# Weight loads placed between the activation loads in a projection, attention and feed-forward kernel on eight cores

## The chip, the cores and the metric

The program runs on all 8 NeuronCores of one Trainium2 chip, four on each of its two dies. Every core runs the same instructions on its own half of a batch entry. The metric is the device time of the slowest core in microseconds (us). Each core has five engines, called here PE (matmuls), DVE (vector), ACT (activations), POOL and SP; SP does no arithmetic and issues most of the transfers.

## The reference, cut to what matters

```python
def attn(x, Wqk_w, Wqk_b, Wv_w, Wv_b, Wo_w, Wo_b):      # x: (4, 4096, 4096), seen as 8 heads of 64
    qk = (x @ Wqk_w.T + Wqk_b).reshape(b, n, H, E, 2)
    q, k = qk[..., 0], qk[..., 1]                       # heads in front
    v = (x @ Wv_w.T + Wv_b).reshape(b, n, H, E)
    scores = einsum('bhqd,bhkd->bhqk', q, k)
    attn = softmax(scores, axis=-1) / sqrt(512)
    out = einsum('bhsl,bhlv->bhsv', attn, v)
    return out @ Wo_w.T + Wo_b
x = layernorm(x + attn(x))
x = layernorm(x + ffn(x))     # ffn: x @ W_base.T + b_base, plus 8 low-rank experts of which 2 are mixed in
```

## The kernel before, in words

A core holds one batch entry: all 4096 tokens for keys and values, and 2048 of them for queries and for everything behind the attention. Activations lie transposed, with the 4096 features along the partitions in 32 chunks of 128.

The kernel writes its program through a small recording layer (class Sched, line 56). `s.op(engine, function, waits, dma=stream)` appends an instruction to the engine's list, in the order in which the Python code comes to it, and puts semaphore waits in front of it. An engine works through its list in that order, so an instruction of SP that waits holds up every transfer that SP issues behind it. A DMA stream ("ld", "sc", three semaphores each) also makes a transfer wait for the third one before it in that stream. `Res` keeps who wrote and who reads a buffer. `phase_barrier` (line 73) ends a stage: all engines meet, and the next stage's first instructions wait for all transfers.

The stages that the change touches, in order:

- **Keys** (lines 306 to 386). The weight wkT comes first, by `wload` (line 199): 32 loads of 256 KB by SP (line 208) into two staging buffers `wstg`, each cast to bf16 by DVE (line 214) into `wk_bf`. Then, for 16 groups of 256 tokens and 8 groups of 4 feature chunks, SP loads x (line 331, 512 KB, three buffers `xstg`), POOL or ACT in turn casts it (lines 343 and 338), ACT sends the cast to the scratch tensor xscr in memory (line 348), and PE does 16 matmuls with it. One pass over the 8 groups is a contraction; ACT then moves its result to `kT` (line 381).
- **Values** (lines 390 to 457). The same with wvT: 16 loads of 512 KB into two buffers, cast by DVE; then 16 passes of 8 loads of 256 KB from xscr (line 416) and 64 matmuls.
- **Queries** (lines 461 to 518). 16 loads of wqT as for the values; then 4 passes of 8 loads of 512 KB (line 480) and 128 matmuls.
- **Attention** (lines 522 to 837). First SP loads the output weight woT in 16 pieces of 512 KB through one buffer `wstgo` (line 548); POOL casts each (line 555) to `wo_bf`. Then come 16 groups (4 head pairs by 4 groups of 512 queries). For each query the maximum of its scores is found first: PE computes scores `sS`, DVE reduces them (line 593), PE transposes the maxima (line 618), DVE writes them as rows `mrow` and `mtmp` (line 631), and SP copies `mtmp` to partition 64 of `mrow` (line 647). Then PE computes the scores again into `rb`, adds the negative maxima by a matmul with `mrow`, ACT takes the exponential (line 739), and PE multiplies by the values. The score and maximum work of the next group (list `units`) is handed out in small pieces between the steps of the present one (`drain_n`); what is left of it is issued by `drain_until` when the next group begins.

`wo_bf` is read only in the stage after the attention. The feed-forward stages behind it are not touched.

## Time and profile before

| What | us |
|---|---|
| time, median of 2 runs (lowest to highest) | 4124.35 (4116.83 to 4131.87) |
| the profiled execution, its own time | 4120.41 |
| span of its slowest core, core 7 (first to last instruction) | 4117.0 |
| span of its fastest core, core 4 | 4054.7 |
| PE busy on core 7 | 3156.3 (77%) |
| DVE, ACT and POOL busy | 1401.7, 829.5, 671.2 |

The rows come from one profiled execution, on core 7 unless the group says otherwise. Times count from the span's start. PEld is PE's weight load, which runs beside its matmuls. In the slices the span is cut into 40 equal parts, and each digit is the busy share in tenths. In the rows of stretches PEclk is the share of its full clock that PE was granted, and the DMA share is the mean of the core's 16 DMA engines. A name like "SPq" stands for issuing a transfer on SP's queue; the transfer itself lands later.

### The profile page before, as it was taken

The page shows a single profiled execution, that of the slowest core. Times are in us where ns is not written, and L with a number is a line of the kernel's source. Part 1 is how long each engine was busy: PE and PEld are TensorE (multiplying, and loading weights), DVE is VectorE, ACT ScalarE, POOL GpSimd, SP SyncE. Part 2 cuts the span into 40 slices and gives each one's busy share as a digit, 9 for nine tenths or more (in the row PEclk, how much of TensorE's full clock was granted, in tenths as well). Part 3 has the DMA queues.
Part 4 walks back from the last instruction along what each step waited for, and adds up shares of the span by engine and source line. Part 5 has one row for each costly group of instructions (what it writes and reads, how often), then busy time and mean ns, then how long its engine had stood idle before and what let it go on. Part 6 is the DMA issues. An engine that isn't in the chain of part 4 may idle for free.

```text
span 4117.0 us, 46517 instructions; the slowest of 8 cores (4054.7 to 4117.0 us)
## 1 busy us (share of the span) xinstructions
PE 3156.3 (77%) x13476; PEld 1181.6 (29%) x13476; DVE 1401.7 (34%) x1972; ACT 829.5 (20%) x1412; POOL 671.2 (16%) x543
## 2 busy tenths in 40 slices
PE   2766499586888887888888887742899997999950
PEld 1555234231222221222212222111344442444420
DVE  1000100115666666565655637771100002111123
ACT  0222000001333333333333343220000000000000
POOL 0111000001000000000000003453222212444425
PEclk9999799795777766777866779986899998999975
DMA  6999544432000000000000012316454536677737
GB/s 180 278 278 278 178 133 136 156 123 62 1 1 1 4 1 1 3 1 1 1 3 1 1 49 96 104 58 184 129 160 146 159 105 194 205 203 209 204 112 184
DMA packets 451280, 444.76 MB, mean 108 GB/s; under 512 B 22112, under 2 KB 403169, under 8 KB 451042
## 3 DMA queue, kind: packets, MB, share of 16 engines
q1 hardware_dynamic: 348130, 341.12, 28.5%
q10 hardware_dynamic: 102912, 100.68, 7.8%
q8 instruction: 123, 2.02, 0.2%
q14 instruction: 115, 0.94, 0.1%
HBM read 340.01 MB, written 100.66 MB: 107 GB/s over the span
## 4 chain that ended last, share of the span: by engine, by line
PE 54%; DVE 8%; issue 6%; DMA 5%; POOL 3%; SPq 0%; ACT 0%; DVEq 0%; POOLq 0%; ACTq 0%
PE pf L155 24%; PE sS L155 10%; PE rb L155 9%; PE a L155 7%; DVE racc L593 3%; DMA res2d<-r2scr 2%; DVE x2g L997 2%; POOL tmpf L987 2%; PE po L155 2%; DMA wstgo<-woT 1%; POOL tmpo L1137 1%; PE pss L155 1%; PE sS L618 1%; PE psq L155 1%; DVE res L934 1%
## 5 line engine op out<-in xcount | busy, mean ns | idle before, releaser
L155 PE MATMUL pf<-x2h,wqf 128*128 128x512 bf16 x4096 | 909.1, 380 | 5.8 <-DVE hs L1333 5.8
L593 DVE TENSOR_REDUCE racc<-sS 128x1 f32<-128x512 f32 x1024 | 682.0, 689 | 529.3 <-PE sS L155 517.9
L739 ACT ACTIVATE probs<-rb 128x512 bf16<-128x512 f32 x1024 | 543.4, 600 | 914.4 <-PE rb L155 910.4
L155 PE MATMUL sS<-kT,qT 64*128 64x512 bf16 x1024 | 476.0, 483 | 152.5 <-DVE racc L593 115.7
L155 PEld LDWEIGHTS pf<-x2h,wqf 128*128 128x128 bf16 x4096 | 396.6, 98 | 505.1 <-issue 38.5
L987 POOL TENSOR_TENSOR tmpf<-res,abc 128x512 f32<-128x512 bf16 x128 | 158.5, 1254 | 1653.8 <-DVE abc L968 1599.5
L155 PE MATMUL pk<-xbf,wk_bf 128*128 128x256 bf16 x2048 | 254.9, 277 | 177.9 <-POOL xbf L343 103.9
L1424 DVE SCALAR_TENSOR_TENSOR res2c<-pf,bB_sb,x2h 128x1024 bf16<-128x1024 f32 x64 | 82.2, 1284 | 864.4 <-PE pss L155 781.2
L1358 POOL CAST wqf<-wstgf 128x1024 bf16<-128x1024 f32 x256 | 264.5, 1040 | 613.6 <-DMA wstgf<-wbT 450.0
L155 PE MATMUL a<-probs,V 128*65 128x512 bf16 x1024 | 363.1, 480 | 0.0
L155 PE MATMUL rb<-qT,kT 64*128 64x512 bf16 x1024 | 337.9, 472 | 0.2
L155 PE MATMUL rb<-mrow,ones 1*128 1x512 bf16 x1024 | 246.6, 468 | 41.0 <-DMA mrow<-mtmp 41.0
L155 PE MATMUL pv<-wv_bf,xvb 128*128 128x512 bf16 x1024 | 229.8, 382 | 62.7 <-DMA xvb<-xscr 47.7
L155 PEld LDWEIGHTS pk<-xbf,wk_bf 128*128 128x128 bf16 x2048 | 195.1, 99 | 237.5 <-issue 210.6
L1442 ACT ACTIVATE sqc<-res2c 128x1024 bf16<-128x1024 bf16 x64 | 67.7, 1058 | 951.7 <-DVE res2c L1424 923.2
L155 PEld LDWEIGHTS sS<-kT,qT 64*128 64x128 bf16 x1024 | 98.0, 96 | 510.2 <-issue 506.2
L155 PE MATMUL po<-OT,wo_bf 128*128 128x512 bf16 x512 | 141.6, 406 | 69.9 <-DVE res L934 64.2
L1137 POOL TENSOR_TENSOR tmpo<-res2d,a 128x1024 f32<-128x1024 bf16 x64 | 155.0, 2439 | 241.3 <-DMA res2d<-r2scr 126.4
L155 PEld LDWEIGHTS a<-probs,V 128*65 128x65 bf16 x1024 | 107.2, 130 | 172.8 <-issue 149.1
L155 PE MATMUL pq<-xqb,wq_bf 128*128 128x512 bf16 x512 | 116.2, 388 | 51.8 <-DMA xqb<-xscr 47.0
L155 PEld LDWEIGHTS pv<-wv_bf,xvb 128*128 128x128 bf16 x1024 | 99.0, 98 | 193.3 <-issue 84.9
L997 DVE TENSOR_TENSOR x2g<-tmpf,bbc 128x512 bf16<-128x512 f32 x128 | 141.2, 1134 | 34.0 <-POOL tmpf L987 33.5
(104 smaller groups left out, 1603.8 us busy)
## 6 DMA issues: line engine op xcount, KB each, us to landing
wstgf<-wbT SPq DMA_DIRECT2D x256, 512.0 KB
xstg<-xrot SPq DMA_DIRECT2D x128, 512.0 KB
xscr<-xbf ACTq DMA_DIRECT2D x128, 256.0 KB, 5.5
xvb<-xscr SPq DMA_DIRECT2D x128, 256.0 KB, 2.8
outT<-outst ACTq DMA_DIRECT2D x64, 512.0 KB, 5.4
xqb<-xscr SPq DMA_DIRECT2D x32, 512.0 KB, 3.7
xq<-xscr SPq DMA_DIRECT2D x32, 512.0 KB, 3.9
x2scr<-x2g ACTq DMA_DIRECT2D x32, 512.0 KB, 2.8
```

The lines of the kernel that those rows point to most:

```text
L155: return lambda e: e.matmul(o, l, r, start=st, stop=sp, skip_group_check=True)
L593: e.reduce_max(d, srd, AX.X, negate=True),
L618: idn=id32[:]: e.transpose(o, i, idn),
L739: e.activation(d, srd, AF.Exp),
L934: e.scalar_tensor_tensor(d, a, b, c2, ALU.add, ALU.add),
L987: e.tensor_tensor(d, a, b, ALU.mult),
L997: e.tensor_tensor(d, a, b, ALU.add),
L1137: b=a2[:]: e.tensor_tensor(d, a, b, ALU.mult),
L1358: e.tensor_copy(d, srd),
L1424: e.scalar_tensor_tensor(d, a, b, c2, ALU.add, ALU.add),
L1442: e.activation(d, a, AF.Square),
```

## The change

`wjobs` does what `wload` did, but returns a list of functions, each of which records one load and its cast. The activation loops call four of these after every activation load until the list is empty, so that the 32 weight loads stand between the first 8 activation loads of each projection. The staging buffers become three of 256 KB each in all three projections; for values and queries that makes 32 loads out of 16. The weight of the keys uses the stream "sc" (its x loads use "ld"), those of values and queries "ld". The 16 loads of woT become a list too, and one is recorded at the start of each attention group.

```diff
+    def wjobs(dst_bf, dstR_list, src_dram, stg, stgR, n_chunks, cw,
+              eng="DVE", dma="ld"):
+        src_r = src_dram.ap().rearrange("(c p) n -> p c n", p=128)
+        per = stg[0].shape[1] // cw
+        nb = len(stg)
+
+        def mk(g):
+            def f():
+                st_i = g % nb
+                src = src_r[:, per * g:per * g + per, :]
+                tl = s.op("SP", lambda e, d=stg[st_i], src=src, per=per:
+                          e.dma_start(d.ap().rearrange(
+                              "p (c n) -> p c n", c=per), src),
+                          waits=stgR[st_i].wr(), dma=dma)
+                stgR[st_i].did_write(tl)
+                tc = s.op(eng,
...
+                          waits=[tl])
+                stgR[st_i].did_read(tc)
+                for j in range(per):
+                    dstR_list[per * g + j].did_write(tc)
+            return f
+        return [mk(g) for g in range(n_chunks // per)]
...
-                    wstg = [sbP("wstg%d" % i, [128, 512], F32) for i in range(2)]
-                    wstgR = [Res(), Res()]
+                    wstg = [sbP("wstg%d" % i, [128, 512], F32) for i in range(3)]
+                    wstgR = [Res(), Res(), Res()]
...
-                    wload(wk_bf, wkR, wkT, wstg, wstgR, 32, 512,
-                          eng="DVE", stripe=True)
+                    wkj = wjobs(wk_bf, wkR, wkT, wstg, wstgR, 32, 512,
+                                eng="DVE", dma="sc")
...
                                 xstgR[bi].did_write(tl)
+                                for _ in range(4):
+                                    if wkj:
+                                        wkj.pop(0)()
...
-                    wstg = [sbP("wstgv%d" % i, [128, 1024], F32) for i in range(2)]
-                    wstgR = [Res(), Res()]
+                    wstg = [sbP("wstgv%d" % i, [128, 512], F32) for i in range(3)]
+                    wstgR = [Res(), Res(), Res()]
...
-                    for hh in range(4):
-                        for c in range(4):
-                            st_i = 0
+                    def mk_woj(hh, c):
+                        def f():
...
+                        return f
+                    woj = [mk_woj(hh, c) for hh in range(4) for c in range(4)]
...
                             for qg in range(4):
+                                if woj:
+                                    woj.pop(0)()
                                 drain_until(hp * 4 + qg)
```

The values and queries get the same edits as the keys, with `wvj` and `wqj`.

On SP's queue the start of the key stage reads as follows before; wstg is the staging of the weight wkT, xstg that of the activations.

```order
L242 DMA epsc<-c_eps 1x1
L208 DMA wstg<-wkT 128x512 x32
L331 DMA xstg<-xrot 128x4x256 x128
L140 UNCONDITIONAL_BRANCH
L151 UNCONDITIONAL_BRANCH
```

And so with the change; the pair of rows repeats eight times.

```order
L268 DMA epsc<-c_eps 1x1
L357 DMA xstg<-xrot 128x4x256
L231 DMA wstg<-wkT 128x512 x4
...
L357 DMA xstg<-xrot 128x4x256 x120
L140 UNCONDITIONAL_BRANCH
```

All 32 weight loads stood ahead of the first activation load; now an activation load comes first and four weight loads follow each of the first eight. In the value and query stages SP's queue has the same new pattern, with xvb and xqb in the place of xstg.

On SP's queue the attention stage begins as follows before; wstgo is the staging of woT, and mrow<-mtmp is the row of maxima that PE waits for.

```order
L151 UNCONDITIONAL_BRANCH
L548 DMA wstgo<-woT 128x1024 x16
L647 DMA mrow<-mtmp 1x16x32 x4
L833 DMA OT<-OTtmp 64x2048
L647 DMA mrow<-mtmp 1x16x32 x4
```

And so with the change, from the start of the stage to the first transfer behind the first head pair.

```order
L151 UNCONDITIONAL_BRANCH
L582 DMA wstgo<-woT 128x1024
L683 DMA mrow<-mtmp 1x16x32
L582 DMA wstgo<-woT 128x1024
L683 DMA mrow<-mtmp 1x16x32
...
L871 DMA OT<-OTtmp 64x2048
```

One load of woT stands ahead of each mrow transfer, where all 16 stood ahead of the first.

## Rows read from the trace of the kernel before

**Rows 1.** The span in 40 slices: busy tenths of PE and of the DMA engines.

```profile
PE   2766499586888887888888887742899997999950
DMA  6999544432000000000000012316454536677737
```

**Rows 2.** Busy time by stretches of the first three stages.

```profile
core 7: us, PE busy (x) PEld busy (x) DVE busy (x) ACT busy (x) POOL busy (x), PEclk, DMA share, GB/s
20.00:60.00 40.00, 0.00 (x0) 0.00 (x0) 9.82 (x23) 0.00 (x0) 0.00 (x0) 1.00 0.50 151
60.00:80.00 20.00, 8.97 (x64) 6.90 (x64) 1.28 (x3) 3.40 (x3) 3.12 (x3) 1.00 0.84 240
160.00:360.00 200.00, 140.44 (x1141) 107.13 (x1140) 0.00 (x0) 51.19 (x71) 37.45 (x36) 0.99 0.98 279
440.00:472.00 32.00, 0.00 (x0) 0.00 (x0) 9.02 (x13) 0.00 (x0) 0.00 (x0) 0.50 0.61 199
540.00:700.00 160.00, 150.51 (x677) 64.02 (x676) 0.00 (x0) 10.90 (x20) 0.00 (x0) 1.00 0.47 135
...
820.00:900.00 80.00, 77.52 (x357) 34.66 (x356) 0.00 (x0) 4.86 (x8) 0.00 (x0) 1.00 0.44 138
```

**Rows 3.** Timeline of the key stage: start us, us, what [idle before <-releaser].

```profile
9.10 53.55 SPq L208 DMA_DIRECT2D wstg<-wkT  x32
...
62.70 64.45 SPq L331 DMA_DIRECT2D xstg<-xrot  x24
...
66.84 0.43 DVE L214 CAST wk_bf<-wstg 128x512 bf16<-128x512 f32 x1 [2.38 <-DMA wstg<-wkT]
68.27 1.04 POOL L343 CAST xbf<-xstg 128x1024 bf16<-128x1024 f32 x1 [56.91 <-DMA xstg<-xrot]
...
69.56 7.06 PE L155 MATMUL pk<-xbf,wk_bf 128*128 128x256 bf16 x48 [69.56 <-POOL xbf L343]
...
92.31 0.93 PE L155 MATMUL pk<-xbf,wk_bf 128*128 128x256 bf16 x7
```

**Rows 4.** DMA issues: operation, count, KB each, median us to landing.

```profile
wstg<-wkT SPq DMA_DIRECT2D x32, 256.0 KB, 2.8
wstgv<-wvT SPq DMA_DIRECT2D x16, 512.0 KB, 4.4
...
mrow<-mtmp SPq DMA_DIRECT2D x16, 1.0 KB, 1.6
```

**Rows 5.** Timeline of the value stage's start.

```profile
435.13 38.09 SPq L208 DMA_DIRECT2D wstgv<-wvT  x16
...
479.81 15.33 PE L155 MATMUL pv<-wv_bf,xvb 128*128 128x512 bf16 x64 [47.00 <-DMA xvb<-xscr]
```

**Rows 6.** Timeline of the query stage's start.

```profile
735.51 38.51 SPq L208 DMA_DIRECT2D wstgq<-wqT  x16
...
780.86 30.50 PE L155 MATMUL pq<-xqb,wq_bf 128*128 128x512 bf16 x128 [46.99 <-DMA xqb<-xscr]
```

**Rows 7.** Timeline of the attention stage's start.

```profile
904.34 81.21 SPq L548 DMA_DIRECT2D wstgo<-woT  x16
...
972.70 0.28 DVE L631 CAST mtmp<-sS 1x128 bf16<-1x128 f32 x1 [0.73 <-PE sS L618]
...
985.65 0.62 SPq L647 DMA_DIRECT2D mrow<-mtmp  x1
...
989.57 0.58 PE L155 MATMUL rb<-mrow,ones 1*128 1x512 bf16 x1 [15.90 <-DMA mrow<-mtmp]
```

**Rows 8.** Stretch 990:2300 and score matmuls: core 3 (lowest clock), then core 4 (highest).

```profile
990.00:2300.00 1310.00, 1100.93 (x3733) 273.58 (x3733) 780.45 (x1221) 473.56 (x892) 0.00 (x0) 0.70 0.01 1
L155 PE MATMUL sS<-kT,qT x1024: 372/387/631, 900.3 to 2393.0; 64*128 64x512 bf16 x171
990.00:2300.00 1310.00, 1083.69 (x3789) 275.68 (x3787) 800.99 (x1246) 480.49 (x908) 0.00 (x0) 0.73 0.01 1
L155 PE MATMUL sS<-kT,qT x1024: 372/387/632, 900.1 to 2358.9; 64*128 64x512 bf16 x171
```

More of the change, by code:

```diff
@@ L218, in wload @@
                 dstR_list[per * g + j].did_write(tc)
+    def wjobs(dst_bf, dstR_list, src_dram, stg, stgR, n_chunks, cw,
[13 more added lines that the diff above has]
+                tc = s.op(eng,
+                          lambda e,
+                          d=dst_bf[:, per * g * cw:(per * g + per) * cw],
+                          srd=stg[st_i][:, 0:per * cw]: e.tensor_copy(d, srd),
+                          waits=[tl])
[4 more added lines that the diff above has]
+        return [mk(g) for g in range(n_chunks // per)]
     with ExitStack() as st0:
@@ L400, in build_program @@
                     wvR = [Res() for _ in range(32)]
-                    wstg = [sbP("wstgv%d" % i, [128, 1024], F32) for i in range(2)]
-                    wstgR = [Res(), Res()]
+                    wstg = [sbP("wstgv%d" % i, [128, 512], F32) for i in range(3)]
+                    wstgR = [Res(), Res(), Res()]
                     xvb = [sbP("xvb%d" % i, [128, 1024], BF16) for i in range(4)]
                     xvbR = [Res() for _ in range(4)]
-                    wload(wv_bf, wvR, wvT, wstg, wstgR, 32, 512,
-                          eng="DVE", stripe=True)
+                    wvj = wjobs(wv_bf, wvR, wvT, wstg, wstgR, 32, 512,
+                                eng="DVE", dma="ld")
                     with nc.psum_tensor("pv0", [128, 512], F32) as pv0, \
@@ L423, in build_program @@
                                 xvbR[bi].did_write(tl)
+                                for _ in range(4):
+                                    if wvj:
+                                        wvj.pop(0)()
                                 for j in range(4):
@@ L463, in build_program @@
                     wqR = [Res() for _ in range(32)]
-                    wstg = [sbP("wstgq%d" % i, [128, 1024], F32) for i in range(2)]
-                    wstgR = [Res(), Res()]
+                    wstg = [sbP("wstgq%d" % i, [128, 512], F32) for i in range(3)]
+                    wstgR = [Res(), Res(), Res()]
                     xqb = [sbP("xqb%d" % i, [128, 2048], BF16) for i in range(3)]
                     xqbR = [Res() for _ in range(3)]
-                    wload(wq_bf, wqR, wqT, wstg, wstgR, 32, 512,
-                          eng="DVE", stripe=True)
+                    wqj = wjobs(wq_bf, wqR, wqT, wstg, wstgR, 32, 512,
+                                eng="DVE", dma="ld")
                     with nc.psum_tensor("pq0", [128, 512], F32) as pq0, \
@@ L488, in build_program @@
                                 xqbR[bi].did_write(tl)
+                                for _ in range(4):
+                                    if wqj:
+                                        wqj.pop(0)()
                                 for j in range(4):
@@ L540, in build_program @@
                     rbcR = [Res(), Res()]
-                    for hh in range(4):
-                        for c in range(4):
-                            st_i = 0
+                    def mk_woj(hh, c):
+                        def f():
                             src_ = woT.ap()[c * 128:(c + 1) * 128,
                                             hh * 1024:(hh + 1) * 1024]
-                            tl = s.op("SP", lambda e, d=wstgo[st_i], src=src_:
+                            tl = s.op("SP", lambda e, d=wstgo[0], src=src_:
                                       e.dma_start(d[:], src),
-                                      waits=wstgoR[st_i].wr(), dma="ld")
-                            wstgoR[st_i].did_write(tl)
+                                      waits=wstgoR[0].wr(), dma="ld")
+                            wstgoR[0].did_write(tl)
                             tc = s.op("POOL",
@@ L554, in build_program @@
                                               c * D + hh * 1024 + 1024],
-                                      srd=wstgo[st_i][:]: e.tensor_copy(d, srd),
+                                      srd=wstgo[0][:]: e.tensor_copy(d, srd),
                                       waits=[tl])
-                            wstgoR[st_i].did_read(tc)
+                            wstgoR[0].did_read(tc)
                             woR[c][hh].did_write(tc)
+                        return f
+                    woj = [mk_woj(hh, c) for hh in range(4) for c in range(4)]
                     with nc.psum_tensor("sS", [128, 1024], F32) as Sg, \
```

## The prediction

> **What bounds the kernel now.** I read the slices of the span first, then the busy time by stretches, then the timeline at the four places where a stage begins, and last the issues of the DMA queues. In the slices [rows 1] the reader is to see that PE is not equally busy: it has a 2 in slice 1, and a 4 and a 5 in slices 5 and 8, while the DMA row falls from 9 to 5 and 4 once the first stage is over. So the kernel has no one bound. The key projection is bound by its transfers: from 160 to 360 us the DMA engines are busy 0.98 of the time while PE works 140 of 200 us [rows 2]. The value and query projections are bound by PE: 150.5 of 160 us and 77.5 of 80 us, at a DMA share of 0.47 and 0.44 [rows 2].
>
> Between them lie the gaps that the change is about. At the start of each projection SP issues all loads of the weight first, in two staging buffers, and the activations stand behind them on the same queue. For the keys the 32 weight loads hold SP from 9.10 to 62.70 us, and PE's first matmul comes at 69.56 [rows 3]; for the values SP is held 38.09 us and PE starts at 479.81 [rows 5]; for the queries 38.51 us and 780.86 [rows 6]. In these gaps the DMA engines are busy only 0.50 and 0.61 of the time [rows 2]: a load waits for a cast, and the cast for the load. In the attention stage 16 loads of wo through one buffer hold SP for 81.21 us; a row of maxima that is ready at 972.98 is sent at 985.65 only, and PE sits idle 15.90 us for it [rows 7].
>
> **The change part by part.** All four edits reorder SP's queue; no matmul is added or removed. For the projections I work out how long the first pass over the contraction takes, in which the weight now arrives: 32 weight loads of 256 KB and 8 activation loads. Two limits hold for it.
>
> The first is the time of the DMA engines. One weight load costs 0.50 x 40 us = 20.0 us for 151 GB/s x 40 us = 23 loads, or 0.87 us, in the first gap, and 0.80 us from 0.61 x 32 us and 199 GB/s in the second [rows 2]; I take 0.84. A group of activations costs, with its write to xscr, 0.98 x 200 us over 279 GB/s x 200 us / 786 KB = 71 groups, 2.76 us, in the key stage; 0.47 x 160 us over 82 loads, 0.91 us, for the values; 0.44 x 80 us over 21 loads, 1.67 us, for the queries [rows 2]. The first pass needs 32 x 0.84 = 26.9 us for the weight and 22.1, 7.3 or 13.4 us for eight groups: 49.0, 34.2 and 40.3 us.
>
> The second is the ring of staging buffers. With two buffers 32 loads took 53.55 us [rows 3], a turn of 3.35 us for two; with three, if the turn stays, 32 / 3 x 3.35 = 35.7 us, which hides behind or beside the first limit. Neither limit is reached alone. I take the DMA share that three buffers reached when the x loads began to stream, 0.84 from 60 to 80 us [rows 2]: 49.0 / 0.84 = 58.3, 40.7 and 48.0 us. To each I add 2.8 us from the first issue to its landing [rows 4], 0.4 us for the last cast [rows 3], and the matmuls of the last group, 1.9 us for keys and values (15.33 us / 8 [rows 5]) and 3.8 us for queries (30.50 / 8 [rows 6]).
>
> Keys: 9.1 + 58.3 + 2.8 + 0.4 + 1.9 = 72.5 us for the end of the first pass, which stood at 92.31 + 0.93 = 93.2 [rows 3]: -20.7 us. After it the x loads set the pace as before. Values: 435.1 + 40.7 + 2.8 + 0.4 + 1.9 = 480.9 against 479.81 + 15.33 = 495.1 [rows 5]: -14.2 us; PE sets the pace after that. Queries: 735.5 + 48.0 + 2.8 + 0.4 + 3.8 = 790.5 against 780.86 + 30.50 = 811.4 [rows 6]: -20.9 us. The gain is less than the gap each time, because the gap's bytes have still to be moved and only the idle share of the engines is won back.
>
> Attention: only one wo load stands ahead of the first mrow transfer now, and the next is behind it. The transfer goes out at 972.70 + 0.28 + 0.2 us and lands 1.6 us later, the median [rows 4], so PE goes on at about 974.8 and not at 989.57 [rows 7]: -14.8 us. In the later groups the order is wo load, mrow, wo load, mrow; each wo load finds its buffer long free, since a group of attention takes tens of microseconds and a load with its cast 81.21 / 16 = 5.1 us [rows 7]. So no mrow is queued behind a waiting load.
>
> What the edits cost. PE now waits in the first pass for each cast of the weight; behind these waits stands all of PE, and nobody else needs it. SP's weight loads wait for casts, and the x loads are queued behind them; that is in the sum as the share of 0.84. Values and queries get 32 casts of 0.43 us instead of 16 longer ones; DVE has nothing else to do there (9.02 us of 32 busy [rows 2]). The 16 wo casts of POOL move under the attention stage, where POOL is idle: 0.00 us busy of 1310 [rows 8]. In the key stage DVE's weight casts now run beside POOL's x casts, which before they did not: the last weight cast came before the first x cast [rows 3]. The bounds are 0 and, if each of the four POOL casts of the first pass (1.04 us [rows 3]) stops DVE once, +4.2 us. I take 0, because DVE is idle most of every turn of the ring. The Trainium skill (SBUF — State Buffer, section "Who interferes with whom") says that a VectorE cast in a two-port mode and a GpSimd instruction lock each other out for a whole instruction. No row of this trace shows the two together; by the rule alone the sum would lose up to those 4.2 us.
>
> The sum is -20.7 - 14.2 - 20.9 - 14.8 = -70.6 us against the profiled execution's own 4120.4 us (span 4117.0 and 3.4 around it), so **4049.8 us**, 1.7% less. That execution is 4 us below the median of the runs shown, 4124.35.
>
> The ends. Fast: the engines are never idle, and in the value stage the ring sets 35.7 us: -30.0, -19.2, -28.6 and -14.8, in all -92.6, 4027.8 us. Slow: the third buffer adds nothing, a weight load lands every 53.55 / 32 = 1.67 us and the activations' engine time comes on top: 75.7, 60.9 and 67.0 us, that is -3.3, +6.0, -1.9 and -14.8, in all -14.0, 4106.4 us. I stay in the middle, nearer the fast end, because the row that shows three buffers in flight (0.84) is the nearest one.
>
> **The rivals.**
> First, faster than I say: the first pass fills the DMA engines as the steady key stage does, at 0.98 [rows 2]. That is the fast end, 4027.8 us, 2.2% less. For it: with x and weight loads together up to six transfers are open. Against it: in every turn a weight buffer stands still for a cast and for SP.
>
> Second, the ring is bound by the round trip and not by the number of buffers: 4106.4 us, no change. For it: a weight load takes 2.8 us to land for 256 KB and 4.4 for 512 [rows 4], so the smaller loads of the change carry less in each round trip. Against it: in the first gap these 2.8 us overlap already, since loads follow each other every 1.67 us [rows 3]. The Trainium skill (DMA: Bandwidth & Descriptors, sections "Anatomy of one DMA — SWDGE (gpsimd) path" and "Bandwidth") speaks against the change here: about 2.0 us fixed for each DMA plus its bytes at 436 GB/s, hence large transfers. As an estimate by that page, 32 x 2.6 - 16 x 3.2 = 32 us more in each of two stages if nothing overlaps, and the sum would be some -6 us; the 1.67 us between landings say that the fixed part overlaps here.
>
> Third, slower: PE's clock in the attention stage. Its granted clock lies between 0.70 and 0.73 there, a mixture of the two levels 1.2 and 2.4 GHz, and the core at 0.70 takes 1492.7 us for its score matmuls where the core at 0.73 takes 1458.8 [rows 8]: 34 us for 0.03. If the casts and loads now spread over the groups break PE's streaks, the stage runs at less. By that slope a mean 0.06 lower uses the gain up (68 us), and one 0.135 lower would make the kernel 2% slower: 0.135 x 34 / 0.03 = 153 us, less 70.6, is 4203 us. Against it: DVE and not POOL is what PE exchanges work with there, and the eight cores of one run all lie within 0.03.
>
> Fourth, the wait comes back: each mrow stands behind a wo load that waits for POOL. Fifteen groups at up to 5.1 us would take back 76 us, 4126 us. The order on SP speaks against it.
>
> **How the numbers follow.** My forecast has a chance of 0.72, the full engines 0.17, the round trip 0.07, the clock 0.03, the returning wait 0.01. The range leaves out the outer half of the fast case and most of the round trip: 4027 to 4090 us. A measurement of this kernel can tell about 2%, 82 us, from no change. Faster by more than that are the fast case and the lower edge of the forecast, 0.22; slower needs the whole of the third case, 0.02; within 2% the rest, 0.76.
>
> **What would show it.** In the profile after: PE's first key matmul near 15 us, the first pass of keys over near 73 us and DMA shares of 0.8 to 0.9 from 12 to 70 us; the value pass over 46 us after its stage begins (60 now), the query pass after 55 (76 now); PE's wait for the first mrow about 1 us and not 15.90; attention from its first matmul on as long as before. I am wrong if the DMA share of these stretches stays at 0.6 (round trip), if it reaches 0.98 (full engines), or if the attention stage's clock differs by more than 0.02 from before.

## The result, and the profile after

| What | us |
|---|---|
| time after, median of 11 runs (lowest to highest) | 4097.23 (4063.77 to 4222.69) |
| time before, median of the 10 runs beside them | 4152.02 (4116.83 to 4406.00) |
| ratio of the undisturbed runs, 95% interval | 0.9882 (0.9836 to 0.9929) |
| the profiled execution after: its own time, span (core 7) | 4090.63, 4089.1 |

Runs in which the cores of a die ran at a lower clock over the whole span, the profiled ones of wo_only and wo_mid among them, are left out of every ratio and every mean of the attention stage, and where too few are left no ratio is given. The ratio is a gain of 0.0118 x 4120.4 = 49 us (29 to 68), at a forecast of 70.6. The median, 4097.23, lies above the upper end of the range, 4090; by the ratio the profiled execution of before would become 4071.8. So the direction is right, a time within 2% of before is right, and about two thirds of the forecast gain came.

One profiled execution is not enough to say where the rest went, because the executions of one kernel differ in the attention stage by as much as is missing. I therefore profiled before and after twice more (runs before_again, before_third, after_again, after_third, with the kernels unchanged; before_again against the other runs of before has a ratio of 1.001 (0.9974 to 1.0046), and after_again 0.989 (0.9702 to 1.0078)) and cut each core's trace at the same instructions. The table is my own sum over the trace: means over the eight cores, in us.

| Stage | before, 3 executions | after, 3 executions | difference | predicted |
|---|---|---|---|---|
| keys, first pass over | 91.8, 89.5, 89.3 | 72.5, 71.6, 71.6 | -18.3 | -20.7 |
| keys, whole stage | 430.3, 423.4, 418.1 | 417.0, 413.6, 404.7 | -12.2 | -20.7 |
| values, first pass | 65.7, 65.7, 65.4 | 57.1, 56.4, 54.6 | -9.6 | -14.2 |
| values, whole stage | 300.7, 300.6, 300.2 | 292.8, 292.5, 291.1 | -8.4 | -14.2 |
| queries, whole stage | 168.4, 168.8, 167.9 | 150.1, 150.9, 149.2 | -18.3 | -20.9 |
| first score matmul to first mrow | 85.0, 84.7, 84.9 | 70.3, 70.5, 70.4 | -14.5 | -14.8 |
| from there to the last value matmul | 1441.2, 1452.4, 1435.6 | 1465.3, 1472.3, 1463.7 | +24.0 | 0 |
| mean span | 4096, 4076, 4051 | 4044, 4060, 4026 | -31 | -70.6 |

In each cell the executions stand in the order first, again, third. Only the third pair is known to be of one chip (chip 5): before_again ran on chip 8 and after_again on chip 13, and the chip of the first pair is not on record. The mean spans of the third pair differ by 25 us, its attention stages by 28.

Four gains are there, two of them nearly at their forecast. What is missing is two fifths of the values' gain, some of the keys' gain behind their first pass, and above all 24 us that the attention stage became longer.

The slices of the span after, PE, PE's granted clock and the DMA engines, answer to [rows 1]:

```profile
PE   4666699778887978888888897671799997999980
PEclk7999799976666576675656778995899998999995
DMA  7999644620000000000000003324555544666636
```

PE's gaps are smaller: in slices 1, 5 and 8 the 2, 4 and 5 became 4, 6 and 7, and the DMA engines have 7, 6 and 6 there for 6, 5 and 4. Over the attention (from slice 10 on) the DMA row stays at 0, although loads of wo now lie there, and PE's clock has 5 to 7 in most slices.

The stretches of the first passes after (keys, values, queries) answer to [rows 2]; the columns are those of before:

```profile
core 7: us, PE busy (x) PEld busy (x) DVE busy (x) ACT busy (x) POOL busy (x), PEclk, DMA share, GB/s
12.00:70.00 58.00, 26.55 (x117) 14.40 (x118) 15.12 (x31) 5.52 (x5) 4.59 (x5) 0.63 0.81 241
...
431.00:483.00 52.00, 30.58 (x64) 5.09 (x64) 13.67 (x32) 0.00 (x0) 0.60 (x1) 0.52 0.81 211
...
730.00:780.00 50.00, 33.74 (x127) 11.73 (x128) 12.53 (x30) 0.00 (x0) 0.00 (x0) 0.93 0.79 237
```

The DMA share is 0.81, 0.81 and 0.79, close to the 0.84 I assumed. But the last column must be read beside it. In the value stage the share rose from 0.61 to 0.81 while the bytes rose only from 199 GB/s [rows 2] to 211. A DMA engine that is busy is not a DMA engine at its peak: the same bytes took longer in it.

The key stage's start and the end of its first pass in the timeline answer to [rows 3]:

```profile
9.13 0.38 SPq L357 DMA_DIRECT2D xstg<-xrot  x1
9.56 7.86 SPq L231 DMA_DIRECT2D wstg<-wkT  x4
...
17.10 2.72 PE L155 MATMUL pk<-xbf,wk_bf 128*128 128x256 bf16 x12 [17.10 <-DVE wk_bf L238]
...
73.41 1.01 PE L155 MATMUL pk<-xbf,wk_bf 128*128 128x256 bf16 x4 [1.66 <-DVE wk_bf L238]
```

PE starts at 17.10 where it started at 69.56, and ends the first pass at 74.42 where it was 93.2: 18.8 us. The gap of 52 us is gone, and only 19 us are won, as the prediction said: the gap's bytes still have to be moved.

The DMA issues (count, KB each, median us to landing) answer to [rows 4]:

```profile
xvb<-xscr SPq DMA_DIRECT2D x128, 256.0 KB, 2.9
...
wstg<-wkT SPq DMA_DIRECT2D x32, 256.0 KB, 4.5
...
mrow<-mtmp SPq DMA_DIRECT2D x16, 1.0 KB, 1.6
```

A key weight load now takes 4.5 us to land, against 2.8 before.

The value stage's start in the timeline answers to [rows 5]:

```profile
430.73 0.38 SPq L445 DMA_DIRECT2D xvb<-xscr  x1
431.15 4.86 SPq L231 DMA_DIRECT2D wstgv<-wvT  x4
...
436.06 0.42 SPq L445 DMA_DIRECT2D xvb<-xscr  x1
...
436.44 1.01 PE L155 MATMUL pv<-wv_bf,xvb 128*128 128x512 bf16 x2 [8.03 <-DMA wstgv<-wvT]
...
437.79 4.86 SPq L231 DMA_DIRECT2D wstgv<-wvT  x4
...
482.60 1.01 PE L155 MATMUL pv<-wv_bf,xvb 128*128 128x512 bf16 x2 [0.68 <-DVE wv_bf L238]
```

SP gives out four weight loads in 4.86 us and then one activation load, again and again: 5.3 us for the first round (436.06 - 430.73), 6.1 us in the mean of the eight that make the pass. The second activation load (436.06) stands behind four weight loads, and the fourth of them waits until a cast has emptied one of the three buffers. What SP waits for in this pass says so as a whole; the line has who waited for whom, us in total, times and the longest:

```profile
SPq L121 <- DVE wv_bf L238: 29.0, 25, 3.0
```

Every wait of SP that the view lists from 430 to 483 us is for a cast of the weight, and none for the landing of an earlier transfer.

The query stage answers to [rows 6]:

```profile
723.93 0.36 SPq L512 DMA_DIRECT2D xqb<-xscr  x1
724.35 5.19 SPq L231 DMA_DIRECT2D wstgq<-wqT  x4
729.58 0.43 SPq L512 DMA_DIRECT2D xqb<-xscr  x1
729.97 5.48 PE L155 MATMUL pq<-xqb,wq_bf 128*128 128x512 bf16 x16 [7.77 <-DMA wstgq<-wqT]
...
779.45 1.02 PE L155 MATMUL pq<-xqb,wq_bf 128*128 128x512 bf16 x4 [0.27 <-DVE wq_bf L238]
```

The pass is over 780.47 - 723.93 = 56.5 us after its first load, where 55 were forecast.

The attention stage's start answers to [rows 7]:

```profile
943.08 0.28 DVE L667 CAST mtmp<-sS 1x128 bf16<-1x128 f32 x1 [0.73 <-PE sS L654]
943.44 0.62 SPq L683 DMA_DIRECT2D mrow<-mtmp  x1
...
944.23 0.43 SPq L582 DMA_DIRECT2D wstgo<-woT  x1
...
945.29 0.58 PE L155 MATMUL rb<-mrow,ones 1*128 1x512 bf16 x1 [1.24 <-DMA mrow<-mtmp]
```

The row of maxima goes out 0.08 us after it is written, and PE waits 1.24 us for it instead of 15.90.

The stretch 990:2300 on the core with the lowest clock (core 7) and the one with the highest (core 0), with their score matmuls, answers to [rows 8]:

```profile
990.00:2300.00 1310.00, 1108.20 (x3618) 267.84 (x3616) 758.39 (x1183) 460.09 (x863) 13.52 (x13) 0.67 0.02 7
L155 PE MATMUL sS<-kT,qT x1024: 372/582/631, 874.8 to 2398.6; 64*128 64x512 bf16 x171
990.00:2300.00 1310.00, 1081.06 (x3794) 274.37 (x3793) 799.63 (x1245) 478.37 (x904) 14.59 (x14) 0.73 0.02 7
L155 PE MATMUL sS<-kT,qT x1024: 372/387/631, 858.0 to 2302.1; 64*128 64x512 bf16 x171
```

Before, the cores lay between 0.70 and 0.73; now one is at 0.67, and it is the one that sets the time. Its score matmuls take 1523.8 us and those of core 0 1444.1. The median score matmul took 582 ns on core 7 and 387 on core 0: more of them ran at the lower of PE's two levels, 1.2 and 2.4 GHz. In the mean over cores and executions the stage's clock is 0.72 before and 0.70 after. Summed over the stage, from the first mrow on, PE is busy 1213.7 us before and 1237.6 after (mean of the cores and of the three executions) and idle 229.3 and 229.5. So the whole 24 us are matmuls that took longer, and not waits.

### The profile page after: what moved, and what is told of

Its sections match the earlier page's. It is cut to its first block, busy times and chain, and to the rows that moved or that the text cites. A ratio compares the mean times of both kernels' runs of the same rounds, so it can differ in the third digit from the quotient of the medians.

```text
span 4089.1 us, 46702 instructions; the slowest of 8 cores (3996.5 to 4089.1 us)
## 1 busy us (share of the span) xinstructions
PE 3266.1 (80%) x13476; PEld 1188.5 (29%) x13476; DVE 1416.6 (35%) x2004; ACT 832.7 (20%) x1412; POOL 668.2 (16%) x543
## 4 chain that ended last, share of the span: by engine, by line
PE 57%; DVE 9%; issue 6%; DMA 3%; POOL 3%; DVEq 0%; ACT 0%; SPq 0%; POOLq 0%; ACTq 0%
PE pf L155 24%; PE sS L155 11%; PE rb L155 9%; PE a L155 8%; DVE racc L629 4%; DVE x2g L1035 2%; POOL tmpf L1025 2%; PE po L155 2%; PE pss L155 1%; PE sS L654 1%; DMA res2d<-r2scr 1%; POOL tmpo L1175 1%; DMA wstgf<-wbT 1%; PE psq L155 1%; DVE res L972 1%
## 5 line engine op out<-in xcount | busy, mean ns | idle before, releaser
L155 PE MATMUL sS<-kT,qT 64*128 64x512 bf16 x1024 | 495.4, 507 | 145.8 <-DVE racc L629 115.2
L155 PE MATMUL pk<-xbf,wk_bf 128*128 128x256 bf16 x2048 | 274.6, 290 | 153.8 <-ACT xbf L367 69.6
L155 PE MATMUL a<-probs,V 128*65 128x512 bf16 x1024 | 390.8, 510 | 0.0
L155 PE MATMUL rb<-qT,kT 64*128 64x512 bf16 x1024 | 364.7, 504 | 0.0
L589 POOL CAST wo_bf<-wstgo 128x1024 bf16<-128x1024 f32 x16 | 16.6, 1040 | 1856.0 <-DMA wstgo<-woT 1856.0
L155 PE MATMUL rb<-mrow,ones 1*128 1x512 bf16 x1024 | 261.4, 496 | 29.1 <-DMA mrow<-mtmp 29.1
L155 PE MATMUL pv<-wv_bf,xvb 128*128 128x512 bf16 x1024 | 246.2, 396 | 38.6 <-DVE wv_bf L238 15.7
```

What stands on the lines that cost most here:

```text
L155: return lambda e: e.matmul(o, l, r, start=st, stop=sp, skip_group_check=True)
L589: srd=wstgo[0][:]: e.tensor_copy(d, srd),
```

## The experiments

My theory after the result: (a) the four edits give what the table shows, independently of each other; (b) the values miss because their weight comes through a ring of three buffers, three loads open at a time; (c) attention is longer because something in it changed, and not by the chance of three executions. Rivals: for (b) the DMA engines themselves are full; for (c) the scatter of executions, the earlier first mrow, or what the earlier stages leave behind.

**The parts by themselves.** Run proj_only is the change with all wo loads at the start of attention, as before:

```diff
                     woj = [mk_woj(hh, c) for hh in range(4) for c in range(4)]
+                    for f_ in woj:
+                        f_()
```

> The edits of the three projections alone; the 16 wo loads stand at the start of the attention as before. First passes end as with the whole change (keys 71 to 75 us, queries 18 to 20 us earlier within the stage than before); attention from the first score matmul to the first mrow is 84 to 86 us as before. Theory 1: attention back at a mean of 1441 us and a clock of 0.72, time about 4120 - 20 - 8 - 19 = 4073, ratio 0.988. Theory 2: attention anywhere from 1430 to 1470, no difference to the whole change beyond the 14 us of the first mrow.

Run wo_only is the kernel before with nothing but the list of wo loads, one at the start of each group:

```diff
                             for qg in range(4):
+                                if woj:
+                                    woj.pop(0)()
                                 drain_until(hp * 4 + qg)
```

> The edit of the wo loads alone; the projections are those of before. First mrow about 70 us after the first score matmul instead of 85. Theory 1: attention has a mean of about 1465 us at a clock near 0.70, so that the edit gains 14 and loses 24, ratio 1.002. Theory 2: attention mean about 1441 or wherever this execution falls, ratio 0.996 or 0.997.

Measured: proj_only 0.9938 (0.9893 to 0.9983), where 0.988 was expected. Its key pass ends at 72.2, its value and query stages take 291.0 and 149.6 us, as in the change, and PE's first wait for mrow, on core 7 in the timeline, is there again:

```profile
933.43 0.58 PE L155 MATMUL rb<-mrow,ones 1*128 1x512 bf16 x1 [15.82 <-DMA mrow<-mtmp]
```

The rest of its attention took 1454.5 us, where theory 1 had 1441 and theory 2 anything from 1430 to 1470. wo_only has the projections of before (90.4, 300.5, 167.9) and the first mrow after 70.0 us; its whole time gave no ratio. So the gains of the edits are separate, and the gain at the first mrow is real (14.5 us). What the wo edit alone does to the attention this pair does not show: on cores 0 to 3 of wo_only the stage took 1450 us, no longer than the mean of proj_only on the same chip, and on cores 4 to 7 1474.

**The ring.** Run ring5 gives the weights of the values and queries five staging buffers, and every stream "ld" and "sc" five semaphores:

```diff
-DMA_STREAMS = {"ld": 3, "sc": 3, "sca": 2, "out": 2}
+DMA_STREAMS = {"ld": 5, "sc": 5, "sca": 2, "out": 2}
...
-                    wstg = [sbP("wstgv%d" % i, [128, 512], F32) for i in range(3)]
+                    wstg = [sbP("wstgv%d" % i, [128, 512], F32) for i in range(5)]
```

> The whole change with five staging buffers of 256 KB (and five semaphores in a stream) in the value and query stages instead of three. With the change the value stage's first pass takes 57 us from the end of the stage before to its first eviction, mean of the cores, where 47 were predicted on the same scale. Theory A (the ring's round trip limits it): more loads in flight, DMA share from 0.81 to 0.92 or more, first pass of values 50 us or less and of queries 55 or less (61 with the change). Theory B (the engines themselves take longer for a weight load when activation loads are mixed in, 1.00 us instead of 0.84): both passes stay within 3 us of 57 and 61.

Measured: the value pass 45.4 us for 56.0 and the stage 282.3 for 292.1; the query pass 51.1 for 60.8 and the stage 140.3 for 150.1. Ten us each, and the keys, whose buffers stayed three, are as they were (70.8). The value pass in the stretches of core 7:

```profile
418.00:460.00 42.00, 23.66 (x66) 5.72 (x66) 13.62 (x32) 0.62 (x1) 0.60 (x1) 0.76 0.89 265
```

The engines move 265 GB/s at a share of 0.89 (0.92 or more had been expected), where they moved 211 at 0.81. So they were not full, and what held the pass was the number of weight loads that may be open, with the round trip of each. This kernel raised buffers and semaphores together. That the buffers were the shorter of the two is read from the traces: with the change SP waited in this pass for casts alone, and in ring5 the keys, with five semaphores and still three buffers, gained nothing. By itself the run's ratio is 0.9744 with a wide interval (0.9440 to 1.0048).

**wo out of attention.** Run wo_in_q loads and casts wo in the last three passes of the query stage, in 32 pieces through the queries' staging buffers, and nothing is left of it in attention:

```diff
+                                for _ in range(2 if g % 3 == 2 or g == 7 else 1):
+                                    if qg and woj:
+                                        woj.pop(0)()
```

> The edits of the projections, and the wo weight loaded and cast under the query stage (32 pieces of 256 KB through the three staging buffers of that stage, in its second to fourth pass, cast by POOL), so that nothing of it is left in the attention and the first mrow is not held up. Theory 1: first mrow at 70 us, attention mean 1441 us, time about 4120 - 20 - 8 - 19 - 14 = 4059, ratio 0.985. Theory 2: first mrow at 70 us, attention anywhere from 1430 to 1470 us. A third theory, that the early mrow itself puts the attention in another rhythm: attention mean about 1465 us here too. The query stage keeps its 150 us if the DMA engines, at a share of 0.44 before, hide 8 MB more.

Measured: 0.9906 (0.9835 to 0.9977); the query stage 152.6 (2.3 us more than with the change), the first mrow 70.8, attention 1449.8 at a clock of 0.71. The early mrow alone therefore need not lengthen attention.

**The amount of wo work.** In wo_x8 a group does its wo load and cast eight times, spread over the group; in wo_cast_x8 once the load and eight times the cast.

```diff
+                                wo_g = woj[hp * 4 + qg]
+                                wo_g()
...
+                                    if kp % 2 and kp < 15:
+                                        wo_g()
```

> The whole change, with each wo load and its cast done up to eight times (spread over the group; the same piece into the same place), 122 loads and casts inside the attention instead of 16. So far, means over eight cores: attention from the end of the first mrow wait 1441 and 1452 us with nothing in it (before, twice), 1455 with the projections changed, 1450 with wo under the query stage; 1465 and 1462 with the 16 loads inside. Theory 1 (each load and cast costs the attention 0.5 to 1 us): 106 more of them give 50 to 110 us more, a mean of 1510 to 1575. Theory 2 (the attention only varies by itself): 1440 to 1475.

> The whole change, with each of the 16 casts of POOL done eight times in a row, the loads as they are. Theory 1a (what costs is the cast, which shuts DVE out of SBUF): 112 more casts of 1.04 us give up to 110 us more in the attention, a mean of 1500 to 1575. Theory 1b (what costs is the load): 1465 as with the change. Theory 2: 1440 to 1475, not to be told from 1b.

Measured: attention 1458.2 and 1468.0 us, both on chip 13, where the change took 1472.3. Core 7 of wo_cast_x8 in the stretch 990:2300:

```profile
990.00:2300.00 1310.00, 1085.35 (x3723) 273.54 (x3722) 787.46 (x1225) 470.81 (x889) 116.49 (x112) 0.71 0.02 7
```

Eight times the POOL work (116 us), and as long as the change. So the length does not grow with the amount. In that run 64 of the reductions of scores on core 7 in this stretch lie beside a POOL cast and take 687.7 ns in the mean, the 825 others 688.9. The Trainium skill (SBUF — State Buffer, section "Who interferes with whom") says that a reduction of this kind never contends with GpSimd for the port; here the trace agrees.

**The load that comes back in front of mrow.** In the change PE waits longer for mrow in three groups, the first of head pairs 2 to 4, which the prediction had excluded. SP's queue and PE at the second head pair, core 7 of the change:

```profile
1326.16 0.51 SPq L871 DMA_DIRECT2D OT<-OTtmp  x1
1326.82 0.46 SPq L582 DMA_DIRECT2D wstgo<-woT  x1
1327.39 0.61 SPq L683 DMA_DIRECT2D mrow<-mtmp  x1
...
1331.53 0.58 PE L155 MATMUL rb<-mrow,ones 1*128 1x512 bf16 x1 [6.53 <-DMA mrow<-mtmp]
```

There mrow is issued right behind a 512 KB load, and PE has it 4.1 us after its issue. Run wo_behind records the load behind the group's first maxima:

```diff
-                                if woj:
-                                    woj.pop(0)()
                                 drain_until(hp * 4 + qg)
+                                if woj:
+                                    woj.pop(0)()
```

> The whole change, with each wo load recorded behind the group's mrow transfer instead of ahead of it. With the change PE waits 6.5 us for mrow where a new head pair begins (groups 4, 8 and 12, mean of the cores, in two profiles), and 4.7 to 5.1 us before and where wo is loaded elsewhere: there the mrow transfer is ready to go and the 512 KB wo load lies ahead of it on the queue. Theory 3 (this is what the attention lost): the three waits are 4.4 to 5.2 us again, groups 4, 8 and 12 last 98 us on average and not 100, and the attention's mean falls from 1465 and 1472 to about 1450. Theory 2 (the attention varies by itself, the 5 us of these waits apart): waits as in theory 3, attention anywhere from 1440 to 1470.

Measured, the same place on core 7 of wo_behind:

```profile
1320.88 0.52 SPq L871 DMA_DIRECT2D OT<-OTtmp  x1
1321.50 0.52 SPq L683 DMA_DIRECT2D mrow<-mtmp  x1
1322.17 0.51 SPq L582 DMA_DIRECT2D wstgo<-woT  x1
...
1324.16 0.58 PE L155 MATMUL rb<-mrow,ones 1*128 1x512 bf16 x1 [4.43 <-DMA mrow<-mtmp]
```

Here PE has it 2.7 us after its issue. In the mean of the cores the three waits are 4.4, 5.1 and 5.6 us, against 6.5, 6.5 and 6.6 with the change and 4.7, 5.1 and 5.1 before. The order lengthens these waits by 1.8 + 1.4 + 1.5 = 4.7 us, and that much is shown. But attention stayed at 1463.1 us, and in the change PE idles no longer in the stage as a whole (229.5 us, 229.3 before), so that other waits became shorter by as much: the 24 us lie elsewhere.

**Load or cast, and the moment.** Run wo_loads_only leaves the casts out, wo_casts_only the loads (the casts read one piece over and over), and wo_mid moves the load from a group's start to its middle:

```diff
-                            tc = s.op("POOL",
...
-                            woR[c][hh].did_write(tc)
+                            woR[c][hh].did_write(tz)
```

```diff
-                            tl = s.op("SP", lambda e, d=wstgo[0], src=src_:
...
-                                      waits=[tl])
+                                      waits=[t_wo0] + mrowR[hp_ % 2][1][qg_].rd())
```

```diff
                                 for kp in range(16):
+                                    if kp == 8 and woj:
+                                        woj.pop(0)([te])
```

> The whole change with the 16 wo loads in their places but no cast: wo_bf is set to a constant at the start of the attention, so the output projection is left out in effect. If the load is what lengthens the attention (by its transfer into SBUF or its place on SP's queue): mean 1458 to 1472 us. If the cast is: 1436 to 1454.

> The whole change with 16 casts in their places, each started by the group's mrow transfer, and one load instead of 16 (all casts read the same piece, so the output projection has a wrong weight). If the cast is what lengthens the attention (POOL shutting DVE out while DVE evacuates the group before): mean 1458 to 1472 us. If the load is: 1436 to 1454, and the waits at new head pairs fall to 4.4 to 5.2 us.

> The whole change with each wo load held back until the middle of its group (it waits for the last exponential of step 7), and its cast behind it. If the moment decides, that is if load or cast hurts only where the evacuation of the group before and the new mrow fall together: mean 1436 to 1454 us. If wo work anywhere in the group costs: 1458 to 1472.

Measured: attention 1481.4 us with the loads alone and 1466.7 with the casts alone, on chip 5, where the whole change took 1463.7; ratios 0.9928 (0.9876 to 0.9979) and 0.9850 (0.9801 to 0.9898). Each half alone is as long as both, so neither is needed for it. The three waits at new head pairs are 4.4, 5.1 and 5.1 us with the casts alone and 6.5, 6.7 and 6.5 with the loads alone, which shows once more that the load in front makes them longer. wo_mid gave no ratio, and its attention is among those left out; whether the moment in the group matters stays open.

**Inside or outside.** The last two runs cross the remaining suspects. early_outside is wo_in_q with the unused staging buffer left where it was; late_inside is proj_only with one wo load and cast repeated at the start of groups 1 to 15:

```diff
+                    wstgo = [sbP("wstgo0", [128, 1024], F32)]
```

```diff
                     for f_ in woj:
                         f_()
...
+                                if hp or qg:
+                                    woj[hp * 4 + qg]()
```

> The kernel with the wo loads and casts moved into the query stage, and the buffer of the attention stage's wo loads kept in its place although nothing uses it: first mrow early, no wo work inside attention, the layout of the change. If wo work inside attention is what makes attention longer, the stretch from the first mrow's arrival to the last value matmul is 1436 to 1454 us here. If the layout or the early start does it, 1458 to 1472 us. The first mrow arrives 70 to 71 us after the first score matmul and the wait at each new head pair is 4.4 to 5.1 us either way.

> The kernel with the projections of the change and the attention stage of before (all sixteen wo loads and casts at its start), and besides, at the start of each of groups 1 to 15, one wo load and its cast done once more: first mrow late, wo work inside attention. If wo work inside is what makes attention longer, the stretch from the first mrow's arrival to the last value matmul is 1458 to 1472 us, with a wait of about 6.5 us at each new head pair. If it is the early start, 1436 to 1454 us. The first mrow arrives 84 to 85 us after the first score matmul either way.

Measured: 1457.6 and 1460.8 us, with the first mrow after 70.8 and 84.6 us and waits of 4.4 to 5.1 and of 6.5 us at the new head pairs, as expected. late_inside falls where wo work inside puts it. early_outside falls between the two ranges, above every other kernel without wo work, so that this pair by itself decides nothing.

All profiled executions that can be compared say more; attention from the first mrow to the last value matmul, in us:

| wo work inside attention | executions |
|---|---|
| none behind the first mrow | 1435.6, 1441.2, 1452.4 (before); 1454.5 (proj_only); 1449.8 (wo_in_q); 1444.8, 1442.2 (ring5_wo_in_q, twice); 1457.6 (early_outside): mean 1447.3 |
| spread over the groups | 1463.7, 1465.3, 1472.3 (after); 1452.0 (ring5); 1458.2, 1468.0 (eightfold); 1463.1 (wo_behind); 1481.4, 1466.7 (halves); 1460.8 (late_inside): mean 1465.2 |

The groups differ by 17.9 us; within each the executions scatter by 8 (standard deviation, of 8 and of 10), so the difference is about five times its own uncertainty of 3.7. This counts the executions as alike, but they come from several chips. On chip 5 three without such work took 1435.6 to 1444.8 us and four with it 1463.1 to 1481.4, 28 us apart in the mean. On chip 15 one of each took 1457.6 and 1460.8, which is no difference. On chip 8 only executions without it can be compared, on chip 13 only executions with it. So wo work spread over the groups goes with a longer attention on chip 5, at a lower granted clock (0.70 against 0.72), whatever its kind; chip 13 adds that eight times the amount makes it no longer. On the other chips it is not shown. How so little work lowers the clock no run here shows, and it stays open.

**The better version.** Run ring5_wo_in_q joins the two edits that helped, five deep rings and wo in the query stage; ring5_again is the same kernel in another series.

> The two best parts together: five staging buffers for values and queries, and the wo weight under the query stage through that ring. If the gains are independent: value stage 282 us, query stage 140 to 145 (150 and 153 with three buffers), first mrow at 70, waits at new head pairs 4.4 to 5.2 us, attention 1440 to 1455; mean of the cores about 4010 and ratio about 0.974. If 8 MB of wo on top of five buffers crowd the query stage: query stage 150 or more, ratio 0.977.

> The best version once more, unchanged: value stage 281 us, query stage 142, attention 1436 to 1454, mean of the cores 4000 within 10 us, ratio 0.975 to 0.981.

Measured: 0.9805 (0.9731 to 0.9878) and 0.9804 (0.9748 to 0.9860), where 0.974 and 0.975 to 0.981 had been expected; the value stage 281.0 and 280.2, the query stage 142.3 and 140.8, attention 1444.8 and 1442.2. This kernel is about 2% below before, where the change is 1.2% below; the two intervals overlap a little, and it is the three stages that are clearly shorter than with the change. Its gain is 0.0195 x 4120.4 = 80 us.

## Why the prediction was right or wrong

**Keys: near in size, by a limit that was thought hidden.** 72.5 us forecast for the end of the first pass, 72.5, 71.6 and 71.6 measured, with a DMA share of 0.81 where 0.84 was assumed. But the engines' time did not set the pass; the ring of three staging buffers did, as the table below shows, and that both come to nearly the same here is luck. No run gave the keys more buffers. "After it the x loads set the pace as before" held less well: the rest of the stage took 339, 334 and 329 us before and 345, 342 and 333 after. The chip is a part of it: four kernels with this key stage took 341 to 342 on chip 13. On chip 8 the rest took 334 before and 335 in proj_only and wo_in_q, on chip 5 329 before and 332 to 339 with the change's key stage. What the remaining few us are I have not shown.

**Values: the term that was mis-sized.** The step that failed is the ring: "with three, if the turn stays, 32 / 3 x 3.35 = 35.7 us, which hides behind or beside the first limit". The turn did not stay. Means over the cores and the three executions after, my own sum over the trace, in us:

| Stage | turn of the three buffers | the ring, 32 / 3 turns | forecast for the transfers, from the engines' time |
|---|---|---|---|
| keys | 5.7 | 60.4 | 58.3 |
| values | 4.5 | 48.2 | 40.7 |
| queries | 5.0 | 53.5 | 48.0 |

In all three stages SP issued a weight load 0.3 to 0.4 us after the cast that emptied its buffer, so the ring was never hidden. A turn became longer because a weight load took 4.8, 3.9 and 4.4 us (medians) from its issue to its cast, where the keys had 2.8 before, with two loads open and no activations between them. The values miss most because their forecast lay furthest below the ring. "With x and weight loads together up to six transfers are open" holds for the streams, since weights and activations use different ones in every stage; but of the weight never more than three can be open, for want of buffers. The share did come (0.81), but at a lower rate: 0.81 x 52 us is 42.1 us of engine time; less ten activation loads at 0.91 us, a weight load costs 1.03 us and not 0.84. With five buffers (ring5) the same sum, 0.89 x 42 us less ten loads, gives 0.88. So the second rival, the ring bound by its round trip, was half right for this stage: a weight load came every 4.5 / 3 = 1.5 us, where two buffers gave one every 1.67 us in the keys, so the longer round trip took back most of what the third buffer brought. The stage gained 8.4 us, between the rival's +6.0 and my -14.2. But the number of buffers counts too, as ring5 shows. The Trainium skill (DMA: Bandwidth & Descriptors, section "Anatomy of one DMA — SWDGE (gpsimd) path") has a fixed part in each DMA that POOL (its GpSimd) issues; the loads here are issued by SP. The runs agree in kind, since 256 KB took 2.8 us to land and 512 KB 4.4 [rows 4]; but the estimate in the prediction, which lets nothing overlap (-6 us for everything), is far from the measured 49.

**Queries: nearly right.** -18.3 for -20.9. The share was 0.79 at 237 GB/s. Here too the ring set the pass, 53.5 us for 48.0, and ring5 won 10 us.

**First mrow: right.** -14.5 for -14.8, the wait 1.24 us for "about 1 us".

**Attention: wrong.** The step that failed is "attention from its first matmul on as long as before": +24 us behind the first mrow. "So no mrow is queued behind a waiting load" is true, and beside the point: at a new head pair the load does not wait, it is only in front, and mrow lands later (4.0 us after its issue at the second head pair on core 7, 2.5 in wo_behind). I had seen the order "wo load, mrow" and asked only whether the load waits. That is the fourth rival on a small scale, 4.7 us of longer waits, which PE made up elsewhere. The 24 us themselves are busy time, the third rival's direction, at under a third of the size it needed to use the gain up: a clock of 0.702 for 0.719, which by its slope of 34 us for 0.03 is 20 us. I had set it at 0.03 chance and at a fall of 0.06 or more, and gave a small fall no place in the sum. "The eight cores of one run all lie within 0.03" was read as a steady clock; the executions show that one kernel moves by 17 us in this stage from one execution to the next. What lowered the clock stays open, and the runs tie it to the wo work on one chip only.

**The port.** I took 0 of at most 4.2 us. Each of the four POOL casts of the first key pass did stop a DVE cast once. Core 7 after:

```profile
31.22 1.04 POOL L372 CAST xbf<-xstg 128x1024 bf16<-128x1024 f32 x1 [14.55 <-DMA xstg<-xrot]
31.39 1.48 DVE L238 CAST wk_bf<-wstg 128x512 bf16<-128x512 f32 x2 [3.51 <-DMA wstg<-wkT]
```

The first of the two DVE casts took 1.15 us instead of 0.43, until 0.28 us after POOL was done; in all four cases together 2.3 us of DVE time on this core. The rule of the Trainium skill that I weighed (SBUF — State Buffer, section "Who interferes with whom") holds here, with the trace. It cost little, because DVE is idle most of each round, which was the ground for taking 0.

**The sum.** -12.2 - 8.4 - 18.3 - 14.5 + 24.0 = -29.4 in the three pairs of executions, whose mean spans differ by 31 (53, 16 and 25 by pairs, the second across two chips); the ratio of the runs says 49 (29 to 68). Of the 41 us by which the three pairs miss 70.6, 24 are attention, 8.5 the keys behind and in their first pass, 5.8 the values, 2.6 the queries.

## What to carry to other kernels

Work out a ring of buffers with the round trip that its loads will have among the other transfers, not with the one they had alone: here a turn went from 3.4 us for two buffers to 4.5 to 5.7 for three. Ask what SP waits for (a cast, so a buffer, or a landing) before the DMA engines are taken for the limit, and read their share beside GB/s: a share of 0.81 moved 211 GB/s with three weight buffers and 0.89 moved 265 with five. A small transfer that someone waits for goes in front of a large one on its queue, even where the large one waits for nothing. Where one stage makes up a third of the time and its clock differs by 0.03 between the cores of one execution, profile both kernels several times, on one chip, before a gain of 1% is put down to anything, and keep work out of that stage if there is room for it elsewhere.

## What the runs showed of the hardware that I had not expected

Spreading 16 casts of 1.04 us and 16 loads of 512 KB over 1450 us of attention goes with 18 us more in the mean of all executions, at a granted clock lower by about 0.013 (28 us on chip 5, 3 us on chip 15); eight times the casts costs no more. And the bytes per busy time of the DMA engines are not fixed: 211 GB/s at a share of 0.81 is 260 for a full share in the value pass with three weight buffers, and 265 / 0.89 = 298 with five; before, with weight loads alone, it was 199 / 0.61 = 326 for two of 512 KB and 151 / 0.50 = 302 for two of 256 KB [rows 2]. What sets it no run here takes apart.

A PE that is fed piece by piece is also granted less: in the value stage's first pass its clock was 0.52, and 64 matmuls were busy for 30.58 us where 64 took 15.33 before [rows 5]. It cost nothing that the runs show, since PE waited for casts there.
